# Stores of the W matrix in pairs of windows, and two small tables moved into the memory of other tensors

## The chip, the core and the metric

The kernel is one program on one core of a Trainium2 chip. Its time is the device time of one execution in microseconds (us); the time before is the median of three runs. Five engines work in parallel, each with its own instruction queue: TensorE (PE, with its weight loads listed as PEld), VectorE (DVE), ScalarE (ACT), GpSimd (POOL) and SyncE (SP). SP only starts DMA transfers here. The engines meet at semaphores.

## The reference

A graph of 3125 nodes with 96 features and 103125 directed edges (sorted by target) goes through four layers: a smoothing of ten steps, a gated edge layer, two graph convolutions with a norm, and two weighted graph convolutions. The kernel pads the nodes to 25 tiles of 128. For the first, third and fourth layers it builds two dense matrices, source node by target node: C counts the edges between two nodes, and W sums their weights. In the reference these are the scatter sums

```
agg = jax.ops.segment_sum(h[src], dst, num_segments=n)                 # C
out = jax.ops.segment_sum(h[row] * norm[:, None], col, num_segments=n) # W
```

The change lies in the stage that builds C and W (`build_matrices`). Its products are not touched.

## The kernel before

`build_matrices` runs after `edge_ranges`, which leaves in HBM a table of 100 groups (first edge column, four ends, a flag) and a copy of the source, high weight and low weight of each edge. A window is 8 target nodes (WIN); 16 windows make a node tile (WPT), 4 windows make a group (GW), 25 tiles make 100 groups and 400 windows. A window's product has 200 columns (WC = 8 nodes by 25 source tiles).

For every group, POOL subtracts the group's bases from the edge keys (`columns`, L415 and L421). DVE compares columns with source numbers into the one-hot tile `S` (L492), with keys into `M` (L498), and multiplies `S` by the two weight parts (L504, twice). `S` and `M` have two buffers, so DVE starts group g when PE has ended group g-2 (L528). PE multiplies them window by window (L573) into one of four PSUM banks `win`, C in the first 200 columns and W in the next. It also transposes the tile before (L592). ACT takes both halves out of PSUM: C into `Cblk` (L641), W into `Wwin` (L645), and now and then a transposed piece into `CT` (L632). PE may start window w when ACT has emptied window w-4. SP stores: `W_d` from `Wwin` window by window (L459), `C_d` once in a tile (L461), and at every fourth window it first loads a register from the table and starts the load of a later group's source columns into `sw` (L444). Before L645 ACT waits until the store of four windows ago has landed:

```
act.wait_ge(s_wst[u % 4], j * 64 + u // 4 * 16 + 1)
nc.scalar.activation(Wwin[:, u % 4, :], win[:, u % 4, WC:2 * WC], ACT.Copy).then_inc(s_evac, 1)
```

The loops of the engines differ in length: DVE's body is four groups, ACT's and SP's two tiles, PE's four tiles, and POOL's two groups, after which POOL runs `columns(0, NG)` once more. `Wwin` lies in `spare`, which is the memory of the node features `nodes_x` (hence its name in the trace: L645 writes, and L459 reads, `nodes_x`). `weight` and `smod` lie in the last tile of `CT` until ACT fills that tile at the very end. `nodes_ident` is first written in the next stage, `propagate` (L759).

Of the kernel before, what the change touches and what calls it, by code (L numbers as in the profile page):

```python
# [11 lines left out]
F32, F16, BF16 = mybir.dt.float32, mybir.dt.float16, mybir.dt.bfloat16  # L12
I32, I16 = mybir.dt.int32, mybir.dt.int16
ALU = mybir.AluOpType
ACT = mybir.ActivationFunctionType
AX = mybir.AxisListType

P = 128
N, D, E, DE = 3125, 96, 103125, 64
NT = -(-N // P)  # L20
# [5 lines left out]
NW = NP // WIN  # L26
WPT = P // WIN
WC = WIN * NT
CH = 4
FEW = CH - 1  # L30
GW = 4
NG = NW // GW
GT = 2 * (GW - 1) + CH
FRONT = 2 * (GW - 1)
SWB = 4
SE = 6
NS = 135
LONG = 4
# [9 lines left out]
ETK = FRONT + TCLAMP + GT + 2  # L48
# [4 lines left out]
PARTS = 3  # L53
# [5 lines left out]
EVAC0 = 7  # L59
# [262 lines left out]
                                        add, None, ALU.add).then_inc(s_tables, 1)  # L322


def build_matrices(nc, tab_d, pair_d, key, smod, weight, CT, indeg, spare, C_d, W_d):

# [2 lines left out]
    HALF = WC // 2  # L331
    with ExitStack() as ctx:
        m = Scope(nc, ctx, "build")
        tab = m.sb("tab", [1, NG + 1, GW + 2], I16)
        colsM = m.sb("colsM", [P, HALF, 2], F16)
        colsS = m.sb("colsS", [P, P // 2, 2], F16)
        ident = m.sb("ident", [P, P], F16)
# [1 line left out]
        stride = m.sb("stride", [P, GW], F32)  # L339

        kw = m.sb("kw", [P, 2, CH, GW, 2], F16)
        sw = m.sb("sw", [P, SWB, PARTS, GT, 2], F16)
        words = spare[:, :, :].rearrange("p k f -> p (k f)")
        CW = NP // 2
        Wwin = words[:, CW:CW + 4 * WC].rearrange("p (r c) -> p r c", r=4)
        M = m.sb("M", [P, 2, CH, GW, HALF, 2], F16)
        S = m.sb("S", [P, 2, PARTS, GT, P // 2, 2], F16)
        Cblk = [words[:, 0:CW].bitcast(F16).rearrange("p (k d) -> p k d", d=P), m.sb("Cblk", [P, NT, P], F16)]
# [22 lines left out]
        s_tp = m.sem("tile_transposed")  # L371
        s_ct = m.sem("transposed_out")
        s_cst = [m.sem(f"C_stored{b}") for b in range(2)]
        s_wst = [m.sem(f"W_stored{r}") for r in range(4)]
        block = ctx.enter_context(nc.Block())

        def group_range(eng, regs, g):
# [13 lines left out]
        @block.gpsimd  # L391
        def _(pool):
            small = dict(allow_small_or_imprecise_dtypes=True)

            nc.gpsimd.iota(colsM[:, :, :].rearrange("p a b -> p (a b)"), pattern=[[1, WC]], base=0,
                           channel_multiplier=0, **small).then_inc(s_const, 1)
            nc.gpsimd.iota(colsS[:, :, :].rearrange("p a b -> p (a b)"), pattern=[[1, P]], base=0,
                           channel_multiplier=0, **small).then_inc(s_const, 1)
            nc.gpsimd.iota(rowh, pattern=[[0, P]], base=0, channel_multiplier=1, **small).then_inc(s_const, 1)
            nc.gpsimd.iota(bases[:, 1, :], pattern=[[HALF, GW]], base=-GW * HALF, channel_multiplier=0,  # L400
                           **small).then_inc(s_const, 1)
            nc.gpsimd.memset(stride[:, :], float(GW * HALF)).then_inc(s_const, 1)
            pool.wait_ge(s_const, 5)
            pool.wait_ge(s_tab, 16)
            reg = pool.alloc_register("pool_bound")

            def columns(b, g):

                pool.load([reg], tab[0:1, bass.ds(g, 1), 0:1])
                t = nc.s_assert_within(pool.snap(reg), 0, FRONT + TCLAMP,  # L410
                                       skip_runtime_bounds_check_because="edge_ranges clamps the tables")
                n = g * NCOL
                pool.wait_ge(s_hot, g + 1)
                pool.sem_inc(s_taken, 1)
                nc.gpsimd.tensor_tensor(bases[:, b, :], bases[:, 1 - b, :], stride[:, :], ALU.add).then_inc(s_cols, 1)  # L415
                pool.wait_ge(s_cols, n + 1)
                pool.sem_inc(s_taken, 1)
                for odd in range(2):
                    pairs = kw[:, b, :, :, :].rearrange("p c (i o) z -> p i o c z", o=2)[:, :, odd, :, :]
                    at = bases[:, b, :].rearrange("p (i o) -> p i o", o=2)[:, :, odd]  # L420
                    nc.gpsimd.tensor_tensor(  # L421
                        pairs,
                        key[:, bass.ds(t + 2 * odd, 2 * CH)].rearrange("p (i c) -> p i c", c=CH).unsqueeze(3).to_broadcast([P, 2, CH, 2]),
                        at.unsqueeze(2).unsqueeze(3).to_broadcast([P, 2, CH, 2]), ALU.subtract).then_inc(s_cols, 1)
                pool.wait_ge(s_cols, n + 3)
                pool.sem_inc(s_taken, 1)

            with pool.Fori(0, NG // 2) as pair:
                columns(0, pair * 2)
                columns(1, pair * 2 + 1)  # L430
            columns(0, NG)

        @block.sync
        def _(sp):
            sp.dma_start(tab[:, :, :], tab_d[0:NG + 1, :].rearrange("(o q) b -> o q b", o=1)).then_inc(s_tab, 16)

            reg = sp.alloc_register("sp_bound")

            def columns(b, g):

                sp.load([reg], tab[0:1, bass.ds(g, 1), 0:1])
                t = nc.s_assert_within(sp.snap(reg), 0, FRONT + TCLAMP,
                                       skip_runtime_bounds_check_because="edge_ranges clamps the tables")
                sp.dma_start(sw[:, b, :, :, :].rearrange("p a t z -> p a (t z)"),  # L444
                             pair_d[:, :, bass.ds(t * 2, 2 * GT)]).then_inc(s_sw[b], 16)

            def store(j, b):

                for u in range(WPT):
                    if u % GW == 0:  # L450
                        g = j * (WPT // GW) + u // GW
                        if not isinstance(j, int):
                            sp.wait_ge(s_made, g + 1)
                            sp.sem_inc(s_taken, 1)
                            sp.wait_ge(s_sw[u // GW], j * 16 + 16)
                            sp.sem_inc(s_taken, 1)
                            columns(u // GW, g + SWB)
                    sp.wait_ge(s_evac, j * (2 * WPT) + 2 * u + 2 + EVAC0)
                    sp.dma_start(W_d[bass.ds(j, 1), :, u * WC:(u + 1) * WC].rearrange("o p c -> p (o c)"),  # L459
                                 Wwin[:, u % 4, :]).then_inc(s_wst[u % 4], 16)  # L460
                sp.dma_start(C_d[bass.ds(j, 1), :, :].rearrange("o p c -> p (o c)"),  # L461
                             Cblk[b].rearrange("p k d -> p (k d)")).then_inc(s_cst[b], 16)

            sp.wait_ge(s_tab, 16)
            for b in range(SWB):
                columns(b, b)
            with sp.Fori(0, NT // 2) as pair:
                store(pair * 2, 0)
                store(pair * 2 + 1, 1)
            store(NT - 1, 0)  # L470
            for b in range(2):
                sp.wait_ge(s_cst[b], 16 * (NT // 2 + 1 - b) + 1)
            for r in range(4):
                sp.wait_ge(s_wst[r], 16 * (NW // 4) + 1)

        @block.vector
        def _(dve):
# [73 lines left out]
        def _(pe):  # L551
# [5 lines left out]
            pe.sem_inc(s_ct, 4)  # L557
            for b in range(2):
                pe.sem_inc(s_cst[b], 1)
            for r in range(4):  # L560
                pe.sem_inc(s_wst[r], 1)
            pe.wait_ge(s_tab, 16)
            pe.wait_ge(s_ready, 2)
# [62 lines left out]
        def _(act):  # L626
# [9 lines left out]
            def node_tile(j, b, before):  # L636

                act.wait_ge(s_cst[b], (j - b) * 8 + 1)
                for u in range(WPT):
                    act.wait_ge(s_built, j * WPT + u + 1 + 2 * GW)  # L640
                    nc.scalar.activation(Cblk[b][:, :, u * WIN:(u + 1) * WIN],  # L641
                                         win[:, u % 4, 0:WC].rearrange("p (d k) -> p k d", d=WIN),
                                         ACT.Copy, scale=0.5).then_inc(s_evac, 1)
                    act.wait_ge(s_wst[u % 4], j * 64 + u // 4 * 16 + 1)
                    nc.scalar.activation(Wwin[:, u % 4, :], win[:, u % 4, WC:2 * WC], ACT.Copy).then_inc(s_evac, 1)  # L645
                    if before and u % GW == 2:
                        turned(j - 1, u // GW)

# [1574 lines left out]
def gnn(nc, x, src_cols, dst_cols, dst_rows, attr, w_cols, We, be, Wn, bn, W1, b1, W2, b2,  # L2223
# [10 lines left out]
    with ExitStack() as outer:  # L2234
# [5 lines left out]
        with ExitStack() as inner:  # L2240
            g = Scope(nc, inner, "graph")
            indeg = g.sb("indeg", [P, NT * len(TG)], F32)
            CT = g.sb("CT", [P, NT, NP], F16)
            with ExitStack() as ctx:
                m = Scope(nc, ctx, "edges")
                key = m.sb("key", [P, ETK], F32)
                weight = CT[:, NT - 1, 0:2 * ETK].bitcast(F32)
                smod = CT[:, NT - 1, 2 * ETK:3 * ETK]
                edge_ranges(nc, src_cols, dst_cols, dst_rows, w_cols, tab_d, tabs_d, base_d, row_d, pair_d, key, smod, weight, unscale, CT)
                build_matrices(nc, tab_d, pair_d, key, smod, weight, CT, indeg, xs, C_d, W_d)  # L2250
            propagate(nc, x, xs, CT, indeg, src_cols, We, be, Wn, bn, ident, first, P_d, Q_d)
        wdeg = o.sb("wdeg", [P, NT], F32)
        gated_edges(nc, src_cols, dst_cols, w_cols, attr, We, Wn, tabs_d, base_d, row_d, P_d, Q_d, ident, first, xs, wdeg)
# [43 lines left out]
```

## Time and profile before

| | |
|---|---|
| median of three runs | 2702.98 us (2699.75 to 2709.37) |
| the profiled execution | 2699.71 us |
| its span, first to last instruction | 2697.9 us |
| PE, DVE, ACT, POOL busy, share of the span | 82%, 61%, 50%, 41% |
| the stage that is changed | about 53 to 549 us |
| in it: PE, DVE, ACT, POOL busy | 402.3, 403.6, 298.5, 282.4 us |
| in it: granted TensorE clock, mean DMA share | 0.96, 0.44 |

The profiled execution's own time is 1.8 us more than its span and 3.3 us less than the median. Busy time of an engine is the union of its instructions; idle time is put down to what released the next instruction. A row that says that an engine waited "for issue" found nothing in the profile that it waited for.

### The profile page before, as it was taken

The numbers are of one execution on the slowest core, as the hardware profiler recorded it, in microseconds if no ns is written. First come the engines' busy times: TensorE is split into PE (matmuls) and PEld (weight loads), VectorE is DVE, ScalarE is ACT, GpSimd is POOL, SyncE is SP. The second block draws the span as 40 slices with busy tenths as digits, with TensorE's granted clock in tenths as the row PEclk, the third lists the DMA queues.
The fourth block names the chain that finished last, engine by engine and source line by source line (L and its number), as shares of the span: only waits on it lengthen the run. The fifth ranks groups of instructions, "written<-read, shape, count | busy, mean of one in ns | idle before, by whom it ended". The sixth has DMA issues, their size and how long they took to land. (4 is left out here: it accounts for less than half of the span.)

```text
span 2697.9 us, 55857 instructions
## 1 busy us (share of the span) xinstructions
PE 2221.2 (82%) x18268; PEld 2088.8 (77%) x18269; DVE 1638.3 (61%) x3181; ACT 1356.5 (50%) x2800; POOL 1111.1 (41%) x1225
## 2 busy tenths in 40 slices
PE   2878788869999999687778877788788748779998
PEld 1877777869999999487677777777777648779998
DVE  7888778855433334566565666666666664465465
ACT  1666556643333332165555555555555523257686
POOL 2655556500000000277777777777777702200000
PEclk6999999989999999765555555555555569979999
DMA  1444444410000000444444444444444452096281
GB/s 58 143 131 128 133 128 141 135 45 2 2 2 1 2 2 16 118 118 116 108 113 113 109 117 108 111 115 109 117 109 110 109 213 104 2 385 226 79 292 39
DMA packets 184980, 283.92 MB, mean 105 GB/s; under 512 B 76675, under 2 KB 152678, under 8 KB 179270
## 3 DMA queue, kind: packets, MB, share of 16 engines
q1 hardware_dynamic: 145958, 200.50, 23.4%
q0 software_dynamic: 38688, 79.28, 11.5%
q8 instruction: 171, 2.80, 0.5%
q14 instruction: 163, 1.34, 0.2%
HBM read 210.52 MB, written 69.15 MB: 104 GB/s over the span
## 5 line engine op out<-in xcount | busy, mean ns | idle before, releaser
L1238 POOL DMA_INDIRECT layer_R<-source_terms,layer_srcs x800 | 781.7, 977 | 243.7 <-issue 243.7
L1470 PE MATMUL layer_zp<-layer_right,layer_left 96*128 96x192 f32 x1342 | 471.3, 536 | 178.9 <-DVE layer_left L1257 174.8
L1470 PEld LDWEIGHTS layer_zp<-layer_right,layer_left 96*128 96x128 f32 x1342 | 404.1, 327 | 195.7 <-DVE layer_left L1257 186.7
L1004 PEld LDWEIGHTS layer_acc<-layer_U,graph_CT 128*128 128x128 f16 x6250 | 524.7, 97 | 30.6 <-ACT layer_U L933 21.1
L1004 PE MATMUL layer_acc<-layer_U,graph_CT 128*128 128x192 f16 (+1 forms) x6250 | 529.8, 246 | 22.0 <-ACT layer_U L933 20.0
L573 PE MATMUL build_win<-build_M,build_S 128*128 128x200 f16 x3948 | 382.6, 253 | 127.3 <-DVE build_S L504 77.0
L573 PEld LDWEIGHTS build_win<-build_M,build_S 128*128 128x128 f16 x3948 | 335.3, 99 | 156.9 <-issue 45.6
L1491 PEld LDWEIGHTS layer_acc<-layer_hot,layer_G 128*98 128x98 f32 x1648 | 252.3, 256 | 114.9 <-DVE layer_aggT L1311 114.8
L1491 PE MATMUL layer_acc<-layer_hot,layer_G 128*98 128x32 f32 x1648 | 268.3, 329 | 54.0 <-DVE layer_aggT L1311 53.8
L2209 PE MATMUL layer_acc<-layer_V,layer_turn 128*128 128x96 f32 x2500 | 287.9, 278 | 0.6 <-issue 0.6
L2209 PEld LDWEIGHTS layer_acc<-layer_V,layer_turn 128*128 128x128 f32 x2500 | 286.0, 195 | 0.9 <-issue 0.9
L1416 ACT ACTIVATE layer_y<-layer_R 128x1152 f32<-128x1152 f32 x135 | 156.3, 1158 | 237.3 <-DVE layer_R L1285 237.3
L1285 DVE TENSOR_TENSOR layer_R<-layer_zp,layer_R 128x1152 f32<-128x1152 f32 x135 | 182.4, 1351 | 145.1 <-DMA layer_R<-source_terms,layer_srcs 144.9
L1227 POOL IOTA layer_place<- 128x1 f32 x1 | 0.1, 137 | 577.4 <-POOLq L680 577.4
L1290 DVE SCALAR_TENSOR_TENSOR layer_z<-layer_R,layer_y 128x576 f32<-128x576 f32 (+1 forms) x136 | 102.8, 756 | 213.4 <-ACT layer_y L1423 213.4
L415 POOL TENSOR_TENSOR build_bases<-build_bases,build_stride 128x4 f32<-128x4 f32 x101 | 156.6, 1550 | 181.7 <-DVE build_S L492 179.2
L2137 ACT ACTIVATE layer_turn<-layer_ring 128x2048 f32<-128x2048 f32 x49 | 200.9, 4114 | 30.1 <-PE layer_acc L2209 30.1
L1410 ACT ACTIVATE layer_gate<-layer_z 128x480 f32<-128x480 f32 x135 | 77.6, 574 | 220.7 <-DVE layer_z L1292 220.7
L2065 DVE COPY layer_turn<-layer_ring 128x1152 f32<-128x1152 f32 x49 | 116.8, 2385 | 110.5 <-PE layer_acc L2209 110.3
L824 DVE TENSOR_TENSOR layer_h<-layer_h,layer_acc 128x96 f32<-128x96 f32 x250 | 63.6, 254 | 196.9 <-ACT layer_h L951 193.8
L498 DVE TENSOR_TENSOR build_M<-build_colsM,build_kw 128x3200 f16<-128x3200 f16 x100 | 181.8, 1818 | 1.0 <-issue 0.6
L645 ACT ACTIVATE nodes_x<-build_win 128x200 f32<-128x200 f32 x400 | 137.0, 343 | 83.1 <-DMA W_blocks<-nodes_x 82.0
(312 smaller groups left out, 2890.4 us busy)
## 6 DMA issues: line engine op xcount, KB each, us to landing
layer_ring<-W_blocks SPq DMA_DIRECT2D x41, 1600.0 KB, 8.3
W_blocks<-nodes_x SPq DMA_DIRECT2D x400, 100.0 KB, 2.3
layer_left<-in_attr SPq DMA_DIRECT2D x68, 384.0 KB
layer_C<-C_blocks SPq DMA_DIRECT2D x25, 800.0 KB, 19.8
layer_R<-source_terms,layer_srcs POOLq DMA_INDIRECT x800
C_blocks<-nodes_x SPq DMA_DIRECT2D x13, 800.0 KB, 4.9
C_blocks<-build_Cblk SPq DMA_DIRECT2D x12, 800.0 KB, 4.8
layer_rows<-target_rows SPq DMA_DIRECT2D x68, 96.0 KB
```

The source lines that it names most:

```text
L415: nc.gpsimd.tensor_tensor(bases[:, b, :], bases[:, 1 - b, :], stride[:, :], ALU.add).then_inc(s_cols, 1)
L498: nc.vector.tensor_tensor(M[:, b, :, :, :, :].rearrange("p c i a z -> p (c i) a z"), colsM[:, :, :].unsqueeze(1).to_broadcast(shape), kw[: ...
L573: mm = pe.matmul(out, S[:, b, part, 2 * i + u, :, :].rearrange("p a z -> p (a z)"), M[:, b, u, i, :, :].rearrange("p a z -> p (a z)"), sta ...
L645: nc.scalar.activation(Wwin[:, u % 4, :], win[:, u % 4, WC:2 * WC], ACT.Copy).then_inc(s_evac, 1)
L1004: return pe.matmul(acc[:, k % RING, 0:columns], CT[:, t, k * P:(k + 1) * P], pairs[:, cur, t, 0:columns], start=(t == 0), stop=(t == NT - 1))
L1238: nc.gpsimd.indirect_dma_start(R[:, i, u, :], None, P_d, bass.IndirectOffsetOnAxis(ap=at_u, axis=0)).then_inc(s_R[i], 16)
L1285: nc.vector.tensor_tensor(R[:, i, 0:n, :], zp[h][:, 0:n, 0:D2], R[:, i, 0:n, :], ALU.add).then_inc(s_add, 1)
L1416: nc.scalar.activation(y[:, h, 0:n, :], R[:, i, 0:n, :], ACT.Abs).then_inc(s_abs, 1)
L1470: pe.matmul(out[u], left[:, i, u * P:(u + 1) * P], right[:, i, :], start=(u % 2 == 0), stop=False, skip_group_check=True)
L1491: mm = pe.matmul(acc[h][0:DG, 0:QW], G[:, h, u, :], hot[:, h, u, :], start=(u == 0), stop=(u == last))
L2137: nc.scalar.activation(turn[:, u % RT, 0:KA, :], ring[:, s, :, 0:KA].rearrange("p d k -> p k d"), ACT.Copy).then_inc(s_turn, 1)
L2209: mm = pe.matmul(acc[:, n % 4, 0:D], turn[:, (base + n) % RT, k, :], V[:, i, k, :], start=(k == 0), stop=(k == NT - 1))
```

## The change

W leaves in stores of two windows. They lie in a ring of three pairs: two in the old place of `Wwin`, the third in a tensor of its own, `Wtwo`. The eight pairs of a tile take the places 0, 1, 2, 0, 1, 2, 0, 1 (`WSLOT`), and the next tile begins at place 0 again. ACT waits only ahead of the first window of a pair, SP waits for and stores only the second. Memory for the third pair comes from two moves: the group table `tab` goes into the last tile of `CT`, behind `smod`, and the source columns `sw` go into `nodes_ident` (`later`). POOL's last `columns(0, NG)`, which read the table after the loop, is gone.

```
+WSLOT = (0, 1, 2, 0, 1, 2, 0, 1)
...
-        tab = m.sb("tab", [1, NG + 1, GW + 2], I16)
+        TAB = (NG + 1) * (GW + 2)
+        tab = CT[0:1, NT - 1, 3 * ETK:3 * ETK + TAB].bitcast(I16).rearrange("p (q b) -> p q b", b=GW + 2)
...
-        sw = m.sb("sw", [P, SWB, PARTS, GT, 2], F16)
+        sw = later[:, 0:SWB * PARTS * GT].bitcast(F16).rearrange("p (r a t z) -> p r a t z", r=SWB, a=PARTS, z=2)
...
-        Wwin = words[:, CW:CW + 4 * WC].rearrange("p (r c) -> p r c", r=4)
+        Wtwo = [words[:, CW + 2 * WC * r:CW + 2 * WC * (r + 1)] for r in range(2)] + [m.sb("Wtwo", [P, 2 * WC], F32)[:, :]]
...
-            columns(0, NG)
...
-                    sp.wait_ge(s_evac, j * (2 * WPT) + 2 * u + 2 + EVAC0)
-                    sp.dma_start(W_d[bass.ds(j, 1), :, u * WC:(u + 1) * WC].rearrange("o p c -> p (o c)"),
-                                 Wwin[:, u % 4, :]).then_inc(s_wst[u % 4], 16)
+                    if u % 2 == 1:
+                        sp.wait_ge(s_evac, j * (2 * WPT) + 2 * u + 2 + EVAC0)
+                        sp.dma_start(W_d[bass.ds(j, 1), :, (u - 1) * WC:(u + 1) * WC].rearrange("o p c -> p (o c)"),
+                                     Wtwo[WSLOT[u // 2]]).then_inc(s_wst[WSLOT[u // 2]], 16)
...
-                    act.wait_ge(s_wst[u % 4], j * 64 + u // 4 * 16 + 1)
-                    nc.scalar.activation(Wwin[:, u % 4, :], win[:, u % 4, WC:2 * WC], ACT.Copy).then_inc(s_evac, 1)
+                    r, done = WSLOT[u // 2], WSLOT[:u // 2].count(WSLOT[u // 2])
+                    if u % 2 == 0:
+                        act.wait_ge(s_wst[r], j * (16 * WSLOT.count(r)) + 16 * done + 1)
+                    nc.scalar.activation(Wtwo[r][:, u % 2 * WC:(u % 2 + 1) * WC], win[:, u % 4, WC:2 * WC], ACT.Copy).then_inc(s_evac, 1)
```

The waits at the end of the stage and the semaphores' first counts go from four to three; `gnn` passes `ident` as `later`.

## Rows read from the trace of the kernel before

**Rows 1.** Groups by line, DVE, 53 to 549 us: busy us, mean ns, idle before.

```profile
L498 DVE TENSOR_TENSOR build_M<-build_colsM,build_kw 128x3200 f16<-128x3200 f16 x100 | 181.8, 1818 | 1.0 <-issue 0.6
L504 DVE TENSOR_TENSOR build_S<-build_S,build_sw 128x1280 f16<-128x1280 f16 x200 | 156.8, 824 | 0.0
L492 DVE TENSOR_TENSOR build_S<-build_colsS,build_sw 128x1280 f16<-128x1280 f16 x100 | 82.6, 826 | 85.0 <-PE build_win L573 68.6 <-issue 10.8 <-DMA build_sw<-edge_pairs 4.1
```

**Rows 2.** Waits of all engines, 53 to 549 us: total us, times, longest us.

```profile
ACT nodes_x L645 <- DMA W_blocks<-nodes_x: 82.0, 101, 3.6
...
DVE build_S L492 <- PE build_win L573: 68.6, 36, 8.3
...
PEld build_win L573 <- ACT nodes_x L645: 41.0, 41, 3.2
...
DVE build_S L492 <- issue: 10.8, 9, 1.4
```

**Rows 3.** Timeline of PE and DVE at the end of PE's loop body: start, us.

```profile
154.01 3.59 PE L573 MATMUL build_win<-build_M,build_S 128*128 128x200 f16 x24 [6.42 <-issue]
...
160.20 0.83 DVE L492 TENSOR_TENSOR build_S<-build_colsS,build_sw 128x1280 f16<-128x1280 f16 x1 [7.51 <-PE build_win L573]
...
477.45 0.82 DVE L492 TENSOR_TENSOR build_S<-build_colsS,build_sw 128x1280 f16<-128x1280 f16 x1 [7.77 <-PE build_win L573]
```

**Rows 4.** Timeline of DVE, first instruction of two neighbouring loop bodies.

```profile
426.66 0.82 DVE L492 TENSOR_TENSOR build_S<-build_colsS,build_sw 128x1280 f16<-128x1280 f16 x1 [1.21 <-PE build_win L573]
...
444.06 0.82 DVE L492 TENSOR_TENSOR build_S<-build_colsS,build_sw 128x1280 f16<-128x1280 f16 x1 [1.17 <-issue]
```

**Rows 5.** Waits of ACT in one tile, 432.1 to 449.7 us.

```profile
ACT nodes_x L645 <- DMA W_blocks<-nodes_x: 3.8, 4, 1.2
```

**Rows 6.** Timeline of ACT and DVE around the longest wait for a store.

```profile
297.57 0.34 ACT L645 ACTIVATE nodes_x<-build_win 128x200 f32<-128x200 f32 x1 [3.56 <-DMA W_blocks<-nodes_x]
...
301.95 0.82 DVE L492 TENSOR_TENSOR build_S<-build_colsS,build_sw 128x1280 f16<-128x1280 f16 x1 [2.60 <-PE build_win L573]
```

**Rows 7.** Timeline of SP, 244 to 266 us: start, us from first to last issue.

```profile
249.40 0.58 SPq L444 DMA_DIRECT2D build_sw<-edge_pairs  x1
250.23 2.13 SPq L459 DMA_DIRECT2D W_blocks<-nodes_x  x4
252.56 0.33 SPq L461 DMA_DIRECT2D C_blocks<-build_Cblk  x1
254.76 0.58 SPq L444 DMA_DIRECT2D build_sw<-edge_pairs  x1
```

**Rows 8.** Waits of SP's own queue, 53 to 549 us.

```profile
SPq L459 <- ACT nodes_x L645: 34.8, 45, 1.9
```

**Rows 9.** Line 459, all its stores, from issue to landing in us.

```profile
DMA to landing us min/median/max: 1.6/2.3/4.4
```

**Rows 10.** DMA issues by line, 53 to 549 us: KB each, median us to landing.

```profile
C_blocks<-build_Cblk SPq DMA_DIRECT2D x12, 800.0 KB, 4.8
```

**Rows 11.** The same in the quiet end of the stage, 536 to 549 us.

```profile
W_blocks<-nodes_x SPq DMA_DIRECT2D x9, 100.0 KB, 1.7
```

**Rows 12.** Timeline of ACT over a tile's end (windows 13, 15) and the next head (0, 2).

```profile
249.30 0.34 ACT L645 ACTIVATE nodes_x<-build_win 128x200 f32<-128x200 f32 x1 [0.65 <-DMA W_blocks<-nodes_x]
...
250.97 0.37 ACT L645 ACTIVATE nodes_x<-build_win 128x200 f32<-128x200 f32 x1
...
253.17 0.33 ACT L645 ACTIVATE nodes_x<-build_win 128x200 f32<-128x200 f32 x1
...
255.62 0.33 ACT L645 ACTIVATE nodes_x<-build_win 128x200 f32<-128x200 f32 x1
```

**Rows 13.** Timeline of all engines at the end of the stage.

```profile
538.26 1.25 POOL L421 TENSOR_TENSOR build_kw<-edges_key,build_bases 128x16 f16<-128x16 f32 x2 [0.25 <-POOL build_bases L415]
...
544.83 0.53 SPq L461 DMA_DIRECT2D C_blocks<-nodes_x  x1
...
548.79 2.91 SPq L737 DMA_DIRECT2D nodes_x<-in_x  x5
```

More of the change, by code:

```diff
@@ L322, in _, with build_matrices @@
                                         add, None, ALU.add).then_inc(s_tables, 1)
-def build_matrices(nc, tab_d, pair_d, key, smod, weight, CT, indeg, spare, C_d, W_d):
+def build_matrices(nc, tab_d, pair_d, key, smod, weight, CT, indeg, spare, later, C_d, W_d):
     NCOL = 3
@@ L373, in build_matrices @@
         s_cst = [m.sem(f"C_stored{b}") for b in range(2)]
-        s_wst = [m.sem(f"W_stored{r}") for r in range(4)]
+        s_wst = [m.sem(f"W_stored{r}") for r in range(3)]
         block = ctx.enter_context(nc.Block())
@@ L472, in _ @@
                 sp.wait_ge(s_cst[b], 16 * (NT // 2 + 1 - b) + 1)
-            for r in range(4):
-                sp.wait_ge(s_wst[r], 16 * (NW // 4) + 1)
+            for r in range(3):
+                sp.wait_ge(s_wst[r], 16 * NT * WSLOT.count(r) + 1)
         @block.vector
@@ L559, in _ @@
                 pe.sem_inc(s_cst[b], 1)
-            for r in range(4):
+            for r in range(3):
                 pe.sem_inc(s_wst[r], 1)
@@ L2249, in gnn @@
                 edge_ranges(nc, src_cols, dst_cols, dst_rows, w_cols, tab_d, tabs_d, base_d, row_d, pair_d, key, smod, weight, unscale, CT)
-                build_matrices(nc, tab_d, pair_d, key, smod, weight, CT, indeg, xs, C_d, W_d)
+                build_matrices(nc, tab_d, pair_d, key, smod, weight, CT, indeg, xs, ident, C_d, W_d)
             propagate(nc, x, xs, CT, indeg, src_cols, We, be, Wn, bn, ident, first, P_d, Q_d)
```

## The prediction

> **What bounds the kernel now.** Read the page's busy table and slices first: the change touches one stage, 53 to 549 us of 2697.9. In that stage read the groups by line, for what one group of four windows costs DVE, then the waits of all engines, for what DVE and ACT wait on, then DVE's timeline, for where its gaps lie, and last SP's timeline, since SP issues the stores that change.
>
> DVE is the engine to beat. A group costs it 0.83 + 1.82 + 2 x 0.82 = 4.29 us, 421 us for 100 groups by the groups' busy times [rows 1], of a stage of 496 us. PE is as full (402 us busy, DVE 404). What could be won is therefore not ACT's 82.0 us of waiting for W stores [rows 2], but only the part of it that comes through as idle time of DVE. ACT is fed by PE and has 198 us of slack; PE may run four windows ahead of ACT, and DVE two groups ahead of PE.
>
> DVE idles 68.6 us before L492 for PE, and 10.8 us for nothing that the profile shows [rows 2], 79.4 in all. Two parts of it have nothing to do with W. At each of five returns of PE's four-tile loop PE stands 6.4 us with "issue" as the only reason, and DVE then waits, 7.5 us the first time and 7.8 the last; the five are 37.0 us together [rows 3]. And the first group of each DVE loop body starts some 1.2 us late: 1.17 where "issue" is named, 1.21 where the same gap is put down to PE [rows 4]; nine marked "issue" make 10.8, 1.2 each [rows 2]. There are 24, so 28.8 us. That leaves 79.4 - 37.0 - 28.8 = 13.6 us. This is the ceiling of what earlier stores can give, 0.5% of the kernel.
>
> How much of the 13.6 is the stores' doing? PE's weight loads waited 41.0 us for L645 [rows 2], so some reaches PE. The longest wait for a store, 3.56 us, shows the passage: DVE's next loop start is 2.60 us late, 1.4 more than the usual 1.2, so 40% came through [rows 6]. Elsewhere nothing does: in the tile from 432.1 to 449.7 us ACT waited 3.8 us for stores [rows 5], and the one sizeable DVE gap in it is the ordinary loop start of 1.17 [rows 4].
>
> **The change part by part.** *Stores.* SP is the cause of the late stores. Four stores take 2.13 us to issue, (2.13 - 0.33) / 3 = 0.60 us each; a source load and its gap take 0.83 (249.40 to 250.23), and after C's issue 1.87 us pass before the next load (252.89 to 254.76) [rows 7]. SP waited for ACT at only 45 of 400 stores [rows 8]: at the other 355 the data lay ready and SP was late. Two stores of a group instead of four give SP 1.2 us in each group of about 4.4 us, 120 us over 200 stores. SP then reaches most stores before their data and issues them at once. The first window of a pair now waits for the second, about 1.1 us, but its place is reused six windows later rather than four, except at a tile's head (below). So nearly all of the 82.0 us of ACT's waits should go. DVE gets back between 0 (as in the tile of [rows 5]) and 13.6 us. I take half, 6.8 us: the trace has both examples, and some of the 13.6 is PE itself being as full as DVE.
>
> *A tile's head.* Each tile ends with places 0 and 1 and the next begins with 0 and 1, so pairs 6 and 7 must have landed when windows 0 and 2 come. Today's distances: window 13 ends at 249.64 and window 0 starts at 253.17, 3.53 us; window 15 ends at 251.34, window 2 starts at 255.62, 4.28 us [rows 12]. Needed are SP's reaction, 0.2 us (252.36 to 252.56) [rows 7], and the landing of 200 KB, which the trace does not have. Its neighbours: 100 KB lands after 1.6 to 4.4 us, median 2.3 [rows 9], 1.7 in the quiet end [rows 11]; 800 KB after 4.8 [rows 10]. The slope is (4.8 - 2.3) / 7 = 0.36 us for 100 KB, so 2.7 us at the median, with bounds 1.6 and 4.8 (4.4 + 0.36). 0.2 + 2.7 = 2.9 is under 3.53: mostly no wait. I allow 6 us of ACT waits in all over 24 heads, of which today's share, 6.8 / 82 = 8%, reaches DVE: +0.5 us. Behind a waiting L645 stand ACT's next C eviction and transposes; PE waits for its PSUM bank, then DVE for PE.
>
> The Trainium skill (DMA: Bandwidth & Descriptors, "Anatomy of one DMA") gives about 2.0 us fixed plus bytes over 436 GB/s; 100 KB more would add 0.23 us instead of 0.36, the pair would land after an estimated 2.5 us, and the sum below would be a few tenths of a us lower. No run here shows a 200 KB store yet.
>
> *The end of the stage.* The last pair is stored after window 15, with 100 KB more in front of C's last store, whose issue at 544.83 and landing gate the next stage at 548.79 [rows 13]. Between 0 and 0.36 us; +0.2.
>
> *POOL's last `columns`* ends at 539.51, while the next stage starts at 548.8 [rows 13]: hidden by nine microseconds, worth 0. If that cover were gone it would save about 3 us, never cost any.
>
> *The moves.* The loads of `tab` and `sw` keep their size and order, and the next stage writes `nodes_ident` only after the stage's end. 0. What they could cost is DVE's reading `sw` more slowly at its new place: bounded below by 0, above by half speed on the 300 instructions of L492 and L504, 300 x 0.82 = 247 us [rows 1]. I take 0, since every slice still begins at an even element of the same type. A gain from the moves is excluded: no instruction goes.
>
> Sum: -6.8 + 0.5 + 0.2 = -6.1 us. Against the profiled execution's own 2699.7 this is 2693.6; the median of the runs is 3.3 higher, and on that scale it would be 2696.9. I give **2695 us**.
>
> **The rivals.** *All of it comes back.* Every one of the 13.6 us was a store's doing: 2686. Refilling after PE's five stalls (7.5 against 6.4, 1.1 each [rows 3]) could add 5 more: 2681. For it: the chain of [rows 6], and SP's constant lateness. Against: the tile of [rows 5].
>
> *Hidden anyway.* ACT's waits go and DVE does not notice: 2699.7 + 0.2, on either scale 2697 to 2703. For it: 198 us of ACT's slack, and the full PE.
>
> *Slower: the tile's head.* If 200 KB under load lands late, pairs 6 and 7 hold ACT up at every head, just where DVE's own loop start makes it short. At the 40% of [rows 6], the 6.8 are used up when a head waits 0.7 us, a landing of 4.0 us (4.0 + 0.2 - 3.53). From 4.5 on (waits of 1.17 and 0.42, 24 x 1.59 x 0.4 = 15.3, less 6.6) the kernel is slower by 8.6 us, 2708; at 4.8 it is 2714. For it: the longest landing of 100 KB is already 4.4. Against: the median is 2.3, and less traffic of single stores stands in the queue. It also covers the case that the change fails at its aim, moving ACT's waits to the head instead of removing them.
>
> *Slower: the moved operand.* Half speed on 300 instructions would make 2947 us. Nothing in the rows speaks for it. The Trainium skill (VectorE: DVE Perf Modes, "Mode 2x_1P") asks 4-byte alignment of 16-bit operands for two results a cycle, which the new place keeps; where it did not, that price would fall due. No run shows it.
>
> **How the numbers follow.** The forecast (3 to 10 us won) has 0.50, all of it back 0.25, hidden 0.15, the tile's head 0.09, the operand 0.01. About 0.3%, 8.1 us, is what a measurement of this kernel can tell from no change. Faster by more than that: the 0.25, and 0.15 of the forecast at its lower edge, with the median's scatter, 0.40. Within it: 0.35 + 0.15 = 0.50. Slower: 0.10. The range of 2685 to 2706 leaves out the lower third of "all of it" (0.08) and the two slow cases. The forecast's own range is 2690 to 2700.
>
> **What will show it.** ACT's waits for W stores at L645 well under 30 us, nearly all at a tile's first and third window; SP's stores waiting for ACT at most of 200 issues; 200 KB landing near 2.7 us; DVE's wait for PE before L492 falling from 68.6 to about 62, with the five stalls of PE and 24 loop starts unchanged; L492 and L504 still at 0.82 us. Wrong it would be if the landing is over 4 us, if DVE's sum of gaps stays at 79 though ACT's waits go, or if the five stalls of PE change, which I hold fixed because PE's instructions in its loop are the same.

## The result: slower by 0.34%, with ACT's waits gone

The changed kernel took 2714.25 us (median of nine runs, 2709.71 to 2715.01), the kernel before 2703.76 us in the same hours (2699.41 to 2711.99): ratio 1.0034, interval 1.0021 to 1.0047. The forecast was 2695 us, and the time is outside its range. Two repeats, on two chips, gave 1.0013 (0.9996 to 1.0031) and 1.0015 (1.0000 to 1.0030), so the loss is small and one of the three intervals takes in no change at all.

The change did to its own object what it says. Waits of all engines in the changed kernel, 53 to 556 us (L648 is the old L645, L493 the old L492, L642 the old L641):

```profile
ACT build_Cblk L642 <- PE build_win L574: 115.6, 128, 8.5
ACT nodes_x L642 <- PE build_win L574: 96.5, 141, 10.1
...
DVE build_S L493 <- PE build_win L574: 88.9, 48, 9.5
...
PEld build_win L574 <- ACT nodes_x L648: 39.9, 36, 2.3
...
PEld build_win L574 <- ACT build_Wtwo L648: 10.1, 14, 1.3
...
DVE build_S L493 <- issue: 3.9, 3, 1.4
...
ACT nodes_x L648 <- DMA W_blocks<-nodes_x: 1.0, 1, 1.0
```

In the kernel before, ACT's waits for PE in the same window were:

```profile
ACT build_Cblk L641 <- PE build_win L573: 68.2, 79, 5.5
ACT nodes_x L641 <- PE build_win L573: 46.2, 69, 10.2
```

ACT's waits for stores went from 82.0 us [rows 2] to 1.0. But PE's weight loads wait for L648 no shorter than they did (39.9 + 10.1 us, the second for the pair under a name of its own, against 41.0), and DVE idles 88.9 + 3.9 = 92.8 us before L493 instead of 79.4: 13.4 us more, close to the 13.2 us by which the span grew. ACT now waits for PE in place of the DMA: 115.6 + 96.5 us against 68.2 + 46.2.

SP's queue and line 460, the pair's store, in the changed kernel:

```profile
SPq L460 <- ACT nodes_x L648: 151.2, 98, 7.8
SPq L460 <- ACT build_Wtwo L648: 23.4, 25, 2.0
```

```profile
DMA to landing us min/median/max: 1.9/2.3/4.2
```

SP now waits for its data (L648) at 123 of 200 stores, where it did at 45 of 400 [rows 8]. 200 KB land in 2.3 us at the median, as 100 KB did [rows 9].

DVE's groups by line, changed kernel: the instructions that read the moved operand cost what they cost in [rows 1].

```profile
L505 DVE TENSOR_TENSOR build_S<-build_S,nodes_ident 128x1280 f16<-128x1280 f16 x200 | 156.7, 822 | 0.0
L493 DVE TENSOR_TENSOR build_S<-build_colsS,nodes_ident 128x1280 f16<-128x1280 f16 x100 | 82.7, 827 | 97.8 <-PE build_win L574 88.9 <-DMA nodes_ident<-edge_pairs 4.1 <-issue 3.9
```

Where are the 13.4 us? Sorting the gaps before L492 and L493 as the prediction did, the 24 loop starts grew from 31.7 to 35.6 us, the five gaps at PE's loop returns from 37.0 to 41.8, and all others from 10.6 to 15.4, with three new ones of 1.65, 1.76 and 1.79. (A second profile of the kernel before, below, shows that such sums do not tell the two kernels apart.) One gap of the last kind can be followed. DVE's timeline, then PE's, then windows (the column after POOL is the granted clock), changed kernel:

```profile
127.51 0.83 DVE L493 TENSOR_TENSOR build_S<-build_colsS,nodes_ident 128x1280 f16<-128x1280 f16 x1 [1.65 <-PE build_win L574]
...
130.19 1.57 DVE L505 TENSOR_TENSOR build_S<-build_S,nodes_ident 128x1280 f16<-128x1280 f16 x2
...
137.39 0.83 DVE L493 TENSOR_TENSOR build_S<-build_colsS,nodes_ident 128x1280 f16<-128x1280 f16 x1 [1.65 <-PE build_win L574]
```

```profile
128.05 1.71 PE L574 MATMUL build_win<-build_M,build_S 128*128 128x200 f16 x18
131.91 2.74 PE L574 MATMUL build_win<-build_M,build_S 128*128 128x200 f16 x18 [2.15 <-DVE build_S L505]
```

```profile
122.00:132.00 10.00, 7.49 (x85) 6.70 (x86) 8.23 (x9) 6.38 (x23) 5.63 (x6) 1.00 0.39 117
132.00:136.00 4.00, 4.00 (x31) 3.65 (x31) 3.74 (x4) 1.13 (x4) 2.41 (x3) 0.57 0.69 250
```

DVE starts its loop body at 127.51 after a gap of 1.65 us, so L505 ends late at 131.8; PE, which has worked off its lead, idles 2.15 us for it; the granted clock is then 0.57 on average from 132 to 136 us (between the levels of 2.4 and 1.2 GHz), 18 matmuls take 2.74 us instead of 1.71, and two groups later DVE waits for PE, another 1.65 us.

### The profile page after: what moved, and what is told of

It is laid out like the page before. It is cut to its first block and busy times, and to the rows that moved or that the text cites. A ratio compares the mean times of both kernels' runs of the same rounds, so it can differ in the third digit from the quotient of the medians.

```text
span 2711.1 us, 55093 instructions
## 1 busy us (share of the span) xinstructions
PE 2259.3 (83%) x18268; PEld 2124.7 (78%) x18269; DVE 1637.0 (60%) x3181; ACT 1355.0 (50%) x2800; POOL 1103.9 (41%) x1222
## 5 line engine op out<-in xcount | busy, mean ns | idle before, releaser
L574 PE MATMUL build_win<-build_M,build_S 128*128 128x200 f16 x3948 | 388.2, 255 | 132.2 <-DVE build_S L505 89.6
L574 PEld LDWEIGHTS build_win<-build_M,build_S 128*128 128x128 f16 x3948 | 340.9, 100 | 161.2 <-DVE build_S L505 44.9
L1494 PEld LDWEIGHTS layer_acc<-layer_hot,layer_G 128*98 128x98 f32 x1648 | 273.8, 275 | 110.8 <-DVE layer_aggT L1314 110.3
L1494 PE MATMUL layer_acc<-layer_hot,layer_G 128*98 128x32 f32 x1648 | 289.2, 345 | 47.6 <-DVE layer_aggT L1314 47.6
L417 POOL TENSOR_TENSOR build_bases<-build_bases,build_stride 128x4 f32<-128x4 f32 x100 | 150.8, 1508 | 197.6 <-DVE build_S L493 195.2
L1424 ACT ACTIVATE layer_y<-layer_y 128x1152 f32<-128x1152 f32 x135 | 156.3, 1158 | 4.3
```

The source lines that it names most:

```text
L574: mm = pe.matmul(out, S[:, b, part, 2 * i + u, :, :].rearrange("p a z -> p (a z)"), M[:, b, u, i, :, :].rearrange("p a z -> p (a z)"), sta ...
L1424: nc.scalar.activation(y[:, h, 0:n, :], y[:, h, 0:n, :], ACT.Exp, scale=-1.0).then_inc(s_e, 1)
L1494: mm = pe.matmul(acc[h][0:DG, 0:QW], G[:, h, u, :], hot[:, h, u, :], start=(u == 0), stop=(u == last))
```

## Why a loop start is late

At the end of a DVE loop body a branch leads back. The time from that branch to the next instruction of DVE's queue was worked out from the trace's branch records: 3.46 us at the mean of 24 in the kernel before, of which 1.3 show as idle time because L498 and L504 still run. In it, at every return, two 8 KB packets arrive on the instruction queue; they are taken for DVE's code, since the records name the queue and not the engine. At the return at 450.0 us of the changed kernel the first began 1.04 us after the branch, where an undisturbed one begins at 0.5; the second took 0.90 us, and DVE was back after 3.86. SP's timeline there:

```profile
449.35 0.34 SPq L460 DMA_DIRECT2D W_blocks<-nodes_x  x1
450.74 0.58 SPq L444 DMA_DIRECT2D nodes_ident<-edge_pairs  x1
```

A pair's store is issued 0.65 us ahead of the branch, and its 128 packets of 1600 bytes move from 450.18 to 451.03 us, just as the code is wanted; the first packet of code begins at 451.04. At ten of the twelve returns with a load of over 3.7 us it begins in the same way, within 0.03 us of the end of the store's last packet. At 14 of the 24 returns a store is issued 0.56 to 0.75 us ahead of the branch, and all 12 loads of over 3.7 us are among them; where it is issued 0.89 to 0.97 us ahead, none is. The means of the load are 3.81 us at the first distance and 3.50 at the second; two further profiles of the same kernel have 3.78 and 3.45, 3.79 and 3.46. Before, 2 of 24 took over 3.7. The Trainium skill (Runtime: NRT & Kernel Launch, "Instruction fetch mechanics") says that a taken branch whose target is not in the loaded pages forces a load by DMA before execution goes on; these packets agree. It also says (DMA: Bandwidth & Descriptors, "Queues, rings and completion order") that a DMA engine serves the queues that have work in turn, a whole packet at a time, and that such a packet typically holds 9 to 17 descriptors. The trace agrees only in part: the code comes when the whole store is through and not between two of its 1600-byte pieces. Which pieces make one such packet, and which DMA engine carries the code, the records do not tell, so that code and stores share an engine is inferred from the delay.

Theory F: this collision makes the loss. Its rivals: M, the moved table or operand is slower to read; H, the hand-over in pairs costs; N, the two kernels' scatter.

## Experiments

Ratios are to the kernel before on the same chip, with 95% intervals; "gap" is the mean idle time of DVE at a loop start, "load" the mean time from branch to next instruction, "long" the loads over 3.7 us of 24, "stage" the time from the first L492 to the last.

```
kernel          ratio                    gap   load  long  stage
before, 1st     -                        1.32  3.46   2    481.3
before_again    1.0002 (0.9984-1.0020)   1.47  3.46   0    493.2
moves_only      1.0001 (0.9981-1.0021)   1.43  3.44   1    493.5
single_ring     0.9987 (0.9967-1.0007)   1.33  3.53   3    492.4
split           1.0001 (0.9985-1.0016)   1.34  3.47   1    495.9
no_W            -                        1.18  3.38   0    481.5
after, 1st      1.0034 (1.0021-1.0047)   1.48  3.69  12    494.0
after_again     1.0013 (0.9996-1.0031)   1.45  3.66  12    493.2
after_third     1.0015 (1.0000-1.0030)   1.45  3.65  11    498.0
shift1          0.9993 (0.9980-1.0006)   1.31  3.51   3    485.4
shift1_again    0.9991 (0.9972-1.0010)   1.37  3.58   6    491.6
double_W        1.0068 (1.0048-1.0088)   1.64  3.84  18    504.9
```

**The moves alone.** The new places of `tab` and `sw` and the missing `columns(0, NG)`, with the old `Wwin` and stores.

> The kernel before with the two moves alone (table into the last tile of CT, source columns into the memory of nodes_ident, POOL's last columns gone); W is still stored window by window from four places. Theory F (the pair stores share the DMA engines with the code that DVE loads at each return of its loop; DVE starts late, PE idles, its clock halves): as before, ratio 0.998 to 1.002, mean DVE loop start gap 1.2 to 1.3 us, stage as long as before (first to last L492 481 us, after 494). Rival M (the moved table or the moved operand is slower to read): as after, ratio 1.003, stage about 494 us.

Rival M is out: the ratio is 1.0001 and the load 3.44. But theory F had expected a stage of 481 us and a gap under 1.3; both came out like the changed kernel's. So a stage length or a gap from one profile could not carry the argument, and the kernel before was profiled again (below).

**Single stores into the new ring.**

```
+                    sp.wait_ge(s_evac, j * (2 * WPT) + 2 * u + 2 + EVAC0)
+                    sp.dma_start(W_d[bass.ds(j, 1), :, u * WC:(u + 1) * WC].rearrange("o p c -> p (o c)"),
+                                 Wtwo[WSLOT[u // 2]][:, u % 2 * WC:(u % 2 + 1) * WC]).then_inc(s_wst[WSLOT[u // 2]], 16)
```

> The changed kernel with the ring of three pairs and the waits for a pair kept, but each window stored by itself as soon as it is out (400 stores of 100 KB). Theory F: the code loads meet stores of half the size, the loop start gap falls back to about 1.25 us and the stage to 478 to 484 us, ratio 0.997 to 1.001. Rival H (the hand-over in pairs, the ring of three with its short way back at the tile's head, is what costs): stays at 1.003. Rival P (it is not the size but that SP is now prompt, so that a store always falls on the code load): SP is as busy as before again, so this too goes back; the run with split stores tells P from F.

Ring and waits in pairs are kept, and the loss is gone: H is out in the form that the ring costs. The gap, 1.33, and the stage, 492.4 us, did not follow as F had set them.

**Two halves at the same moment.** As the pair's store, but `for h in range(2)` over its columns.

> The changed kernel with each pair stored at the same moment as in the change, but as two stores of 100 KB, one right behind the other (about 0.6 us apart by SP). Theory F in its narrow form (the burst of 128 packets of 1600 bytes in one store is what the code load has to wait behind): the first half finds the code load half as long in the way, gap 1.25 to 1.4 us, ratio 0.998 to 1.002. Rival P (prompt stores in a fixed phase to DVE's loop): the same bytes in the same phase, gap stays at 1.5 to 1.6 us, ratio 1.002 to 1.005.

The load fell to 3.47 and the ratio to 1.0001, as the narrow form of F expected. But SP had 400 stores again and was late again: ACT waited 87.6 us for them, and the halves mostly left at other distances from the branch than the pair did. So this run does not tell the size of a store from its moment (rival P), and its time settles nothing: the median, 2715.14, is as high as the changed kernel's.

**No store of W in the stage.** SP counts a semaphore in place of the store; `W_blocks` is filled with other numbers in `propagate`.

> The changed kernel without any store of W in the stage: SP stores none, ACT waits for none (W_blocks is filled from CT in the next stage, so the fourth layer works on other numbers). Only the stage from 53 us to the last L492 is to be read. Theory F: without W bursts the loop start gaps are at their floor, 1.15 us or less, no spell of half clock but the five at PE's loop, stage 475 us or less. Rival M or H: the gaps stay above 1.4 us and the stage above 488.

DVE's waits, `no_W`:

```profile
DVE build_S L490 <- PE build_win L571: 64.1, 32, 9.0
DVE build_S L490 <- issue: 17.3, 15, 1.3
```

The gap has its floor here, 1.18 us, and half clock comes, after the start of the stage, at PE's five loop returns alone. But the stage is 481.5 us, not under 475: without all traffic of W a loop start is 0.3 us shorter than in the changed kernel. It also bears on the prediction: without any store 81.4 us of DVE's idle time remain, 28.2 at the loop starts, 42.2 at PE's returns and 11.0 elsewhere. So the residue that the prediction put down to stores is there without them, as far as one profile can say.

**Both kernels again.**

> The changed kernel itself once more, for a second profile and a second ratio. Theory F (pair stores fall on DVE's code load at its loop's return, DVE starts late, PE idles, its clock halves): ratio 1.002 to 1.005 again, mean loop start gap 1.45 to 1.55 us against 1.32 before. Rival N (the difference is where in their scatter the two happened to lie): ratio within 0.9985 to 1.0015, gap no larger than in the kernel before.

> The kernel before itself, as a kernel of its own, for a second profile and for what a ratio of nothing looks like. Both theories: ratio 0.999 to 1.001. Theory F: mean loop start gap 1.3 us again and at most one spell of half clock outside PE's loop ends. Rival N: PE's five loop-end gaps, 37.0 us in the first profile, come out near the 41 us of the changed kernel, so that this part of the difference was the profile's luck.

Waits in the second profile of the kernel before:

```profile
DVE build_S L492 <- PE build_win L573: 83.3, 46, 9.2
ACT nodes_x L645 <- DMA W_blocks<-nodes_x: 82.9, 78, 3.9
```

Rival N is half right. The changed kernel's repeat, 1.0013, lies in N's range and below F's. The first profile of the kernel before was at the low end of its scatter: its own time was 2699.7 us, its runs elsewhere reach from 2698.8 to 2723, and the second profile idles 83.3 us before PE with a stage of 493.2, like the changed kernel. Sorted as above, its gaps are 35.2 us at the loop starts, 40.1 at PE's five returns, near the 41 that N had set, and 15.3 elsewhere, almost the 35.6, 41.8 and 15.4 of the changed kernel; F had expected a mean gap of 1.3 and at most one spell of half clock away from PE's returns; the gap was 1.47, and there were two such spells. The 13 us between the two first spans overstate the loss; the medians say 3 to 10.

Two numbers do not scatter. The load is 3.46 in both profiles, against 3.65 to 3.69 in three of the changed kernel. And the gaps agree once those over 2 us are set aside, at which DVE's code was not late (no load there is over 3.6 us) but PE's work was: 1.27 in both profiles of the kernel before and in `moves_only`, 1.45 to 1.48 in the changed kernel, which has none over 2 us. The clock scatters too: the traces put 38 us of the stage at 1.2 GHz in the first profile of the kernel before and 53 in the second, and 59, 53 and 70 in the three of the changed kernel.

**The dose.** Each pair stored a second time into a tensor that nobody reads.

> The changed kernel with every pair stored twice, the second time into a tensor of its own that nobody reads (W traffic doubled, at the same moments). Theory F (pair stores on DVE's code load cost the time): the loop start gap grows from 1.45 to 1.7 us or more, 6 us or more of time over the changed kernel, ratio to before 1.004 to 1.010. Rival N (the bursts do not matter for the time, the difference to before is mostly scatter): as the changed kernel, ratio 1.000 to 1.004, gap 1.4 to 1.55 us.

Load 3.84, gap 1.64 (a little under what F had set), 18 long loads, ratio 1.0068. ACT also waited some 50 us for the second copies, so not all of the time is the load's.

**The moment.** The store waits for one more eviction, C of the next window:

```
-                        sp.wait_ge(s_evac, j * (2 * WPT) + 2 * u + 2 + EVAC0)
+                        sp.wait_ge(s_evac, j * (2 * WPT) + 2 * u + 2 + EVAC0 + (1 if u < WPT - 1 else 0))
```

> The changed kernel with each pair's store held back until ACT has also taken C of the next window out of PSUM (some 0.7 us later; the last pair of a tile goes as before). Theory F with a fixed phase: the store leaves the start of the code load; the gap moves clearly, below 1.35 us or above 1.6, and the time with it by 3 us or more. Rival N: gap 1.4 to 1.55 us and ratio 1.000 to 1.004 as in the changed kernel.

> The changed kernel beside the held-back one on one chip. Theory F (the pair stores fall on DVE's code loads): mean loop start gap 1.45 to 1.5 us, ratio to before 1.001 to 1.004. Rival N (scatter): ratio and gap not to be told from those of the held-back kernel.

> The kernel with stores held back by one eviction, on the same chip as the changed one. Theory F: gap 1.3 us again, 4 to 10 us faster than the changed kernel (0.15 to 0.35%), ratio to before 0.998 to 1.001. Rival N: within 0.1% of the changed kernel, and its gap of 1.31 was luck.

This is the run that decides on the time. The same bytes in the same packets, some 0.7 us later, and on one chip the medians are 2708.18 us (2703.27 to 2712.64, twelve runs) and 2716.24 for the changed kernel (2713.15 to 2717.82, twelve runs): 8.1 us, with ranges that do not meet. Loads fall to 3.51 and 3.58. DVE's waits in `after_third` and, below it, in `shift1_again`:

```profile
DVE build_S L493 <- PE build_win L574: 94.8, 48, 10.2
```

```profile
DVE build_S L493 <- PE build_win L574: 81.1, 41, 9.6
```

N and H fall as the whole answer: this kernel has the pairs, the ring and the moves, and no loss. It has no gain clear of the noise either, 0.9991 and 0.9993 (0.9972 to 1.0010 and 0.9980 to 1.0006): what it is worth here to take ACT's 80 us away cannot be told from nothing.

That the moment of the store costs the time is shown by this pair; that it does so through DVE's code load is shown for a part. The two profiles' own times differ by 8.0 us. DVE's gaps differ by 7.7: 34.7 against 33.0 us at the loop starts, 46.1 against 42.0 at PE's returns, 16.5 against 14.6 elsewhere. The time at 1.2 GHz is 70 against 55 us. `no_W` has 42.2 us at PE's returns with no store at all, so 46.1 may be scatter.

**Fewer loop returns.** DVE's loop body with 20 groups instead of 4:

```
-            with dve.Fori(0, NG // SWB) as four:
-                for r in range(SWB):
-                    group(r % 2, r, four * SWB + r, four)
+            with dve.Fori(0, NG // 20) as many:
+                for k in range(20):
+                    group(k % 2, k % SWB, many * 20 + k, many * 5 + k // SWB)
```

> The changed kernel with DVE's loop body five times as long (20 groups, 5 turns instead of 25): 20 of the 24 loop returns are gone. Theory F: the place where the pair stores do harm is gone with them; 20 gaps of 1.48 us less, 24 to 30 us won, ratio to before 0.992 to 0.996, and no worse than the kernel before with the same edit. Rival H (the hand-over in pairs costs by itself): it wins less than that kernel by the same 10 us as without the edit.

> The kernel before with the same long DVE loop body. Theory F: 20 gaps of 1.32 us less, but now ACT's 80 us of waits for W stores come through, ratio 0.990 to 0.996, equal to the changed kernel with this edit within 0.2%. Rival H: 10 us faster than the changed kernel with this edit.

> The ring of three pairs with each window stored by itself, and DVE's long loop body: it asks which half of the change made 28 us of difference between the two kernels with that body. Theory S (SP's issue work sets the pace once DVE no longer rests at its loop returns, 400 stores of 0.6 us): ACT still waits 40 us or more for stores, ratio to before 0.999 to 1.004, near the 1.0037 of the old stores. Rival D (the deeper ring alone is enough): ratio 0.993 to 0.996, as with pairs.

The changed kernel gains by it (2692.36 us, 0.9938, 0.9921 to 0.9955), and the kernel before loses by the same edit (2720.64, 1.0037, 1.0017 to 1.0056). That had not been expected; the two were to be equal. Waits of the changed kernel, then of the kernel before, each with the long DVE body:

```profile
DVE build_S L493 <- PE build_win L574: 69.4, 37, 9.9
...
ACT nodes_x L648 <- DMA W_blocks<-nodes_x: 18.1, 23, 2.3
```

```profile
ACT nodes_x L645 <- DMA W_blocks<-nodes_x: 117.3, 81, 3.9
DVE build_S L492 <- PE build_win L573: 99.2, 51, 8.9
...
PEld build_win L573 <- ACT nodes_x L645: 61.5, 52, 3.1
```

With DVE no longer resting at its loop starts, the late single stores come through: ACT waits 117 us, PE's weight loads 61.5 for ACT, and DVE's idle time grows although 20 returns are gone. The whole change is worth 28 us here. The ring alone gives less than half of it: single stores into the new ring take 2708.40 us, 1.0003 (0.9987 to 1.0019), with 108.8 us of waits of ACT. The other 16 us go with 200 stores in place of 400, which agrees with theory S, that SP's issues set the pace; SP waited for its data at 35 of 400 stores in the kernel before with the long body.

**PE's loop too.** `Fori(0, NT // 12)` over 12 tiles in place of `Fori(0, NT // 4)` over 4, on top of the long DVE body.

> The changed kernel with DVE's body of 20 groups and PE's body of 12 tiles instead of 4 (2 turns instead of 6): of the five stalls of PE at its loop's return one is left. If those stalls reach the end in full (DVE's five gaps before PE, 45.0 us in the kernel with the long DVE body), 30 to 36 us more: ratio to before 0.980 to 0.984. If PE's longer body costs code loads of its own on the way, less: 0.984 to 0.994.

> The kernel before with both long bodies. Theory S (single stores keep SP, and through it ACT, PE and its clock, too late once DVE does not rest): ratio to before 0.993 to 1.000, over 1% behind the changed kernel with the same bodies (0.981). Rival: the long PE body heals it too, 0.981 to 0.985.

> Both long bodies and the held-back stores. With four code loads of DVE left instead of 24, theory F has little left to win: within 0.1% of the changed kernel with long bodies, 0.980 to 0.983. If it is over 0.2% better, the stores also fall on code loads inside the long bodies.

The changed kernel with both bodies is the best version: 2657.40 us, ratio 0.9811 (0.9794 to 0.9829), and DVE idles 43.9 us instead of 97.8:

```profile
L493 DVE TENSOR_TENSOR build_S<-build_colsS,nodes_ident 128x1280 f16<-128x1280 f16 x100 | 82.6, 826 | 43.9 <-PE build_win L574 37.5 <-DMA nodes_ident<-edge_pairs 4.0 <-issue 1.3
```

The kernel before with both bodies reaches only 0.9950 (0.9931 to 0.9969), with 172.4 us of ACT's waits. Holding the stores back adds nothing any more: 0.9810.

## Why the prediction was wrong, step by step

- *SP is late, and pairs cure it*: right. SP waits at 123 of 200 stores, and ACT's waits went from 82.0 to 1.0, below the 30 that were set.
- *A tile's head*: one wait of 1.0 us in all, so the slower rival that was named is out; that its 2714 us is what was measured is a coincidence. The landing is 2.3 us, not 2.7; the Trainium skill's fixed part and rate (DMA: Bandwidth & Descriptors, "Anatomy of one DMA"), fitted there to transfers that GpSimd issues while SP issues these, gave an estimate of 2.5, nearer, and the measurement stands.
- *The moves and POOL's last columns, 0*: right as far as can be measured, 1.0001 (0.9981 to 1.0021) alone.
- *"I take half, 6.8 us"*: not borne out. The held-back kernel, with 2.5 and 3.5 us of ACT's waits left, runs as before within the noise, and a residue of 11.0 us stands in the kernel without any store. The 13.6 was also too large in its own trace: nine gaps marked "issue" gave 1.2 us for all 24 loop starts, 28.8, but those measure 31.7, of which 1.4 is the wait of [rows 6], and that leaves about 12.
- *"Two parts of it have nothing to do with W"* is the step that failed. The loop starts were held at 1.2 us because "issue" was their only reason, without asking what an engine waits for there. The trace shows code that comes by DMA, and that comes later when a store of W is under way. SP's lateness had smeared the stores; a prompt SP puts a store twice the size at one place of DVE's loop. So a term that the prediction held at nothing is 3.67 - 3.46 = 0.2 us at each of 24 returns, 5 us, and more where PE then idles and its clock falls.
- *The base*: the argument used one profile at 2699.7 us as if its 79.4 us of idle time were the kernel's. A second profile has 90.6 us of it, and each of the three parts differs by 3 to 5 us between the two, against a forecast of 6.1 in all. So PE's stalls, 37.0 us in the first profile and 41.8 in the changed kernel, are no sign of the change, though the prediction had named them as one: they are 40.1 in the second.

What stays open: how the moment of a store costs what goes beyond the code loads, which are 5 us against the kernel before but only 1.8 of the 8.1 us between the changed kernel and the held-back one on one chip (0.07 us at 24 returns). Half clock after PE's waits is a candidate; no run holds the clock apart from the lateness. Why the kernel before scatters from 2699 to 2723 us was not settled either.

## What to carry to other kernels

An engine that stands "for issue" at a loop's return may be waiting for code, which came later here when a data store was under way: before a store is made larger or more punctual, look where its packets fall against the loop returns, and lengthen the loop bodies first. A wait that is taken away pays only where its engine is late for the bound one; here it was worth nothing that could be measured until most of DVE's own stalls were gone, and 28 us after that. A forecast of 0.2% needs the scatter of the profile that it is made from.

## What the runs showed that was not expected

Removing 20 of DVE's 24 loop returns made the kernel before slower, by 0.37%; the likely reason, by theory S, is that the pauses had given SP the time to catch up. And one kernel's stage lasted 481.3 us in one profile and 493.2 us in the next, a difference larger than the change under study, while the mean code load was 3.46 us in both. Last, a quarter of a microsecond in a store's start decides: issued 0.56 to 0.75 us ahead of the branch a pair goes with a return of 3.8 us at the mean, issued 0.89 to 0.97 us ahead with one of 3.5.
